# Side fetches from lists of byte offsets, read 32 at a time, in a graph network on one core

## The chip, the cores and the metric

The kernel runs on 1 core of one Trainium2 chip. The metric is the device time of one execution in microseconds (us); the kernel before takes 12477.9 us, the median of 3 runs (12459.53 to 12489.42).

## The reference

`h = relu(layernorm(x))` for 12500 nodes of 96 features. Then two mean aggregations over 200000 edges sorted by destination, two edge-conditioned maximum convolutions, and residual additions:

```python
def mean_agg(x):                       # twice; result 0.5*n1 + 0.5*n2, added to x
    return segment_sum(x[src], dst, N) * inv_deg
def _egnn_conv(x, src, dst, edge_attr, W_msg, W_edge, W_root, b):      # twice, with leaky_relu
    msg = x[src] @ W_msg + edge_attr @ W_edge
    agg = segment_max(msg, dst, N)     # 0 where a node has no edge
    return agg + x @ W_root + b
```

Each of the four aggregations needs `x[src]`: 200000 gathered rows of 384 bytes.

## The kernel before, in words

Four rounds follow each other: rounds 0 and 1 are sums, rounds 2 and 3 maxima. A round reads its node table from DRAM (`tables[r]`, 12544 rows of 96 float32), and ends with a stage over the nodes that writes the next table. Edges stand in 391 groups (`GROUPS`) of 512: 4 batches (`GRP`) of 128, one edge per partition.

**The main fetch.** GpSimd (POOL in the profile) issues one indirect DMA per batch (L449), 4 per group: 128 rows by 128 indices of `src_sb`, into a ring `rows` of 8 groups (`RING`). Group g waits until group g - 8 has been consumed (`used`, L441): in a sum when its windows are picked (`picked`), in a maximum when its rows are in PSUM (`rows_ps`). Group g of the ring stands on seat g % 8.

**The consumers.** TensorE takes the groups in order. In a sum it multiplies them with one-hot matrices (L681), and VectorE adds the results to `comp` (L927). In a maximum it multiplies with an identity (L702) on top of the edge features (L700), VectorE scans (L942), TensorE transposes and picks (L713, L724).

**The side fetch.** Some groups don't go through GpSimd: the table `ASIDE` names them. SyncE (SP, side buffer 0) and in the sums also ScalarE (ACT, side buffer 1) fetch each of a group's 512 rows by a DMA of its own (L296) from an address in a register. In `side_rows`, `numbers` (L319) loads 4 row numbers of one partition into registers, and each DMA's address is worked out from one of them. A side buffer holds one group, so the next side group of a queue is begun only when its last one is picked: `side_sums` waits for `picked` and then issues all 512. `PLAN` (9, seat) gives one side group per queue in 9 sweeps of 8 groups: groups 74, 146, 218, 290 and 362 for SP in a sum, 75, 147, ... for ACT, 72, 144, ... for SP in a maximum: 5 of each. TensorE waits for them in `gathered` (L665).

**The last rows.** The edges of the last, partial batch (`REST` = 64 rows) are fetched by SP in `tail_rows` (L302), one number and one DMA at a time, before its first side group of the round.

**SP's other work.** In a sum it stores the table (`store_table`), in a maximum it also loads flags and edge features by units of 4 groups into two buffers (`load_units`, L367 and L369), and side rows are issued between the units. Unit u waits for the scan that frees its buffer.

Of the kernel before, what the change touches and what calls it, by code (L numbers as in the profile page):

```python
# [10 lines left out]
U32 = mybir.dt.uint32  # L31
ALU = mybir.AluOpType
# [14 lines left out]
PLAN = {r: {0: (9, 2), 1: (9, 3)} for r in (0, 1)} | {r: {0: (9, 0)} for r in (2, 3)}  # L47
# [5 lines left out]
SIDES = {r: {e: (SWEEPS - 1) // span for e, (span, _) in PLAN[r].items()} for r in PLAN}  # L53
ASIDE = {r: {(b + 1) * PLAN[r][e][0] * RING + PLAN[r][e][1]: (e, b) for e in PLAN[r] for b in range(SIDES[r][e])} for r in PLAN}
# [14 lines left out]
PREP_ALL = 18  # L69
PREP_MAX = 22  # L70
assert CHUNK * CHUNKS == TILES and CHUNKS % 2 == 0 and RING == 2 * UNIT and UNIT < LAST < RING
assert GRP * (GROUPS - 1) < WHOLE and REST > 0
assert min(seat for _, seat in PLAN[0].values()) >= 2 and all(g < GROUPS - 1 for r in ASIDE for g in ASIDE[r])
# [33 lines left out]
def gnn(nc, x, srcs, cur, prev, nxt, cur_r, prev_r, eat, wm1, we1, wr1, b1, wm2, we2, wr2, b2, out):  # L107
    with ExitStack() as ctx:
# [13 lines left out]
        tables = [nc.dram_tensor(f"table{r}", (NPAD, D), F32).ap() for r in range(ROUNDS)]  # L122

# [14 lines left out]
        base = sb("base", [1, COLS], I32)  # L138
# [93 lines left out]
        side_in = {(r, e): [sem(f"side_rows_landed_{r}_{e}_half{k}") for k in range(2)] for r in rounds for e in PLAN[r]}  # L232
# [40 lines left out]
        def sweeps(engine, r, body):  # L273
# [3 lines left out]
            def passed(i):  # L277

                return {seat: sum(g // RING < i and g % RING == seat for g in ASIDE[r]) for _, seat in PLAN[r].values()}

# [10 lines left out]
        def side_rows(engine, r, e, b, p):  # L291

            span, seat = PLAN[r][e]
            at = bass.ds(b * (span * RING * GRP) + (span * RING + seat) * GRP, GRP)
            for k, row in enumerate(numbers(engine.engine, src_sb[p:p + 1, at], N - 1)):
                engine.dma_start(side[p:p + 1, e, k, 0:D], tables[r][bass.ds(row, 1), :]).then_inc(side_in[r, e][k % 2], 16)  # L296

        def tail_rows(engine, r):

            for p in range(REST):  # L300
                row, = numbers(engine.engine, src_sb[p:p + 1, WHOLE:WHOLE + 1], N - 1)
                engine.dma_start(tail[p:p + 1, 0, 0:D], tables[r][bass.ds(row, 1), :]).then_inc(tail_in, 16)  # L302

        def side_sums(engine, r, e):

            for s in range(2):
                engine.wait_ge(tstored[r][s], 16 * (CHUNKS // 2))
            if e == 0:
                engine.wait_ge(prep, PREP_ALL)
                tail_rows(engine, r)  # L310
            span, seat = PLAN[r][e]
# [15 lines left out]
        def _(sp):  # L327
# [21 lines left out]
            sp.dma_start(next_i, nxt).then_inc(s_next, 16)  # L349

# [10 lines left out]
            def load_units(r):  # L361
# [15 lines left out]
                span, seat = PLAN[r][0]  # L377
                units = 2 * span
                with sp.Fori(0, SIDES[r][0]) as b:
                    sp.wait_ge(rows_ps[r], b * (span * RING) + (seat + 1))  # L380
                    for t in range(units):
                        unit(b * span + (1 + t // 2), t % 2, UNIT)
                        for p in range(t * P // units, (t + 1) * P // units):
                            side_rows(sp, r, 0, b, p)
                with sp.Fori(SIDES[r][0] * span + 1, SWEEPS - 1) as i:
                    for u in range(2):
                        unit(i, u, UNIT)
# [743 lines left out]
```

## Time and profile before

| What | us |
|---|---|
| median of 3 runs | 12477.9 |
| span of the profiled execution, first to last instruction | 8075.9 |
| median less span | 4402.0 |
| GpSimd busy | 5983.3 |
| TensorE busy | 5063.4 |
| VectorE busy | 3315.1 |
| ScalarE busy | 1517.2 |

The page has no time for the profiled execution other than its span, so what lies around it is known only as the difference to the median. Busy times leave out the issue of DMAs by SP and ACT; those rows are marked SPq and ACTq and come from the queries by line. A round's start is seen in GpSimd's rows: the rounds begin at 57.8, 2035.9, 4047.2 and 6072.0 us.

### The profile page before, as it was taken

Reading aid. Unit: us, or ns where it says so; the run is one execution under the profiler, and the core shown is the slowest. Engines: PE = TensorE matmul, PEld = TensorE weight load, DVE = VectorE, ACT = ScalarE, POOL = GpSimd, SP = SyncE. Lnnn points to the kernel's source line nnn. Section 1 sums busy time; section 2 is a strip of 40 time slices with the busy share of each in tenths; the row PEclk is TensorE's granted clock in tenths of the full one; section 3 lists DMA queues with packets and bytes.
Section 4 is the critical chain, followed back from the end, with each engine's and each line's share of the span. In section 5 each row is a group of like instructions: output and inputs, shape, how many; then the busy total and the mean of one; then the engine's idle time right before and its main releaser. Section 6 shows DMA issues by size and latency. Waiting matters only on the chain.

```text
span 8075.9 us, 156597 instructions
## 1 busy us (share of the span) xinstructions
PE 5063.4 (63%) x26211; PEld 3792.9 (47%) x26211; DVE 3315.1 (41%) x7073; ACT 1517.2 (19%) x5246; POOL 5983.3 (74%) x6410
## 2 busy tenths in 40 slices
PE   3444444445444444444677888787787788878878
PEld 2333333334333333333555655565575565556556
DVE  5444444445433333333533433333343343333335
ACT  2000000001000000000322333333342333333334
POOL 6777777776777777777677777777767777777776
PEclk7555555556555555555677888888797787888888
DMA  3111111111211111111144434444433443444443
GB/s 92 42 42 41 42 41 42 41 41 46 57 42 42 41 42 41 41 41 41 41 94 93 98 89 96 93 98 93 92 72 92 97 98 87 97 93 97 93 92 79
DMA packets 337350, 553.38 MB, mean 69 GB/s; under 512 B 212648, under 2 KB 212648, under 8 KB 311848
## 3 DMA queue, kind: packets, MB, share of 16 engines
q0 software_dynamic: 196096, 301.60, 18.2%
q1 hardware_dynamic: 129796, 243.57, 11.9%
q14 instruction: 601, 4.92, 0.2%
q10 hardware_dynamic: 10788, 2.16, 0.2%
q8 instruction: 69, 1.13, 0.1%
HBM read 521.97 MB, written 24.87 MB: 68 GB/s over the span
## 4 chain that ended last, share of the span: by engine, by line
POOL 53%; issue 21%; PE 11%; SPq 9%; DMA 3%; DVE 2%; ACT 1%; DVEq 0%; ACTq 0%; POOLq 0%
POOL rows L449 53%; SPq L296 5%; SPq L319 3%; PE ps L702 3%; PE ps L700 3%; DMA rows<-table,src_sb 2%; PE ps L724 2%; PE ps L807 1%; SPq L302 1%; PE ps L713 1%; DMA arena<-in_eat 1%; PE ps L681 0%; PE ps L818 0%; ACT arena L493 0%; DMA table<-arena 0%
## 5 line engine op out<-in xcount | busy, mean ns | idle before, releaser
L449 POOL DMA_INDIRECT rows<-table,src_sb x6128 | 5790.9, 945 | 1958.6 <-issue 1849.1
L681 PE MATMUL ps<-arena,rows 128*98 128x128 f32 (+1 forms) x6088 | 1513.6, 429 | 2097.1 <-DMA rows<-table,src_sb 1446.2
L681 PEld LDWEIGHTS ps<-arena,rows 128*98 128x98 f32 (+1 forms) x6088 | 1259.8, 276 | 2373.4 <-DVE comp L927 1990.2
L942 DVE TENSOR_TENSOR_SCAN arena<-arena,ps 96x512 f32<-96x512 f32 x782 | 997.6, 1276 | 2433.9 <-PE ps L702 2409.3
L927 DVE TENSOR_TENSOR comp<-comp,ps 98x128 f32 (+1 forms) x3128 | 894.7, 286 | 2158.4 <-PE ps L681 1841.9
L700 PE MATMUL ps<-arena,we 32*96 32x512 f32 x1564 | 993.7, 719 | 765.1 <-DMA rows<-table,src_sb 415.9
L702 PEld LDWEIGHTS ps<-ident,rows 128*96 128x96 f32 x6168 | 823.5, 187 | 714.4 <-issue 714.4
L910 DVE TENSOR_TENSOR arena<-ps,meta 128x512 f32<-128x512 f32 x1564 | 1050.7, 672 | 29.2 <-issue 25.7
L518 ACT COPY comp<-ps 96x128 f32 x3128 | 818.8, 262 | 1057.6 <-PE ps L724 796.4
L702 PE MATMUL ps<-ident,rows 128*96 128x128 f32 x6168 | 1013.5, 316 | 0.0
L724 PE MATMUL ps<-arena 128*96 128x128 f32 x6256 | 932.8, 299 | 0.9 <-ACT arena L509 0.9
L724 PEld LDWEIGHTS ps<-arena 128*96 128x96 f32 x6256 | 829.0, 186 | 1.3 <-ACT arena L509 1.3
L509 ACT COPY arena<-ps 128x384 f32<-128x384 f32 x782 | 373.8, 478 | 1512.3 <-PE ps L713 1500.2
L700 PEld LDWEIGHTS ps<-arena,we 32*96 32x96 f32 x1564 | 210.2, 175 | 902.4 <-DMA rows<-table,src_sb 386.0
L590 ACT COPY arena<-comp 96x128 f32 (+1 forms) x392 | 83.6, 296 | 2064.3 <-issue 1896.1
L713 PE MATMUL ps<-ident,arena 96*128 96x96 f32 x3128 | 454.5, 275 | 0.2 <-DVE arena L942 0.2
L713 PEld LDWEIGHTS ps<-ident,arena 96*128 96x128 f32 x3128 | 392.0, 164 | 0.6 <-DVE arena L942 0.4
L598 ACT COPY rel_c<-node_rel 128x7 f32<-128x7 f32 (+1 forms) x42 | 8.3, 197 | 1742.6 <-issue 1741.4
L463 POOL TENSOR_SCALAR arena<-iota,rel_c 128x128 f32<-128x128 f32 x266 | 179.5, 690 | 123.6 <-ACT rel_c L598 77.8
L915 DVE TENSOR_TENSOR arena<-ps,meta 128x392 bf16<-128x392 f32 x391 | 216.9, 555 | 0.0
L687 PE MATMUL ps<-arena,ones_b 128*1 128x392 bf16 x391 | 185.9, 476 | 0.0
L807 PE MATMUL ps<-arena 128*128 128x96 f32 (+1 forms) x784 | 116.5, 309 | 29.2 <-POOL arena L463 9.3
(104 smaller groups left out, 1404.2 us busy)
## 6 DMA issues: line engine op xcount, KB each, us to landing
side<-table SPq DMA_DIRECT2D x10240, 0.4 KB
arena<-flags SPq DMA_DIRECT2D x194, 768.0 KB
rows<-table,src_sb POOLq DMA_INDIRECT x6128
side<-table ACTq DMA_DIRECT2D x5120, 0.4 KB
arena<-in_eat SPq DMA_DIRECT2D x194, 256.0 KB
table<-arena SPq DMA_DIRECT2D x56, 336.0 KB, 2.8
out<-xs SPq DMA_DIRECT2D x13, 336.0 KB
tail<-table SPq DMA_DIRECT2D x256, 0.4 KB
```

The costliest lines, as they stand in the source:

```text
L296: engine.dma_start(side[p:p + 1, e, k, 0:D], tables[r][bass.ds(row, 1), :]).then_inc(side_in[r, e][k % 2], 16)
L449: pool.indirect_dma_start(rows[:, g % RING, j, 0:D], None, tables[r][:, :], bass.IndirectOffsetOnAxis(src_sb[:, c:c + 1], 0)).then_inc(lan ...
L509: act.copy(runT[:, slot % SCANS].rearrange("p k d -> p (k d)"), ps[:, RUNT + slot % 2 * BANK:RUNT + slot % 2 * BANK + GRP * D]).then_inc(r ...
L518: act.copy(comp[0:D, bass.ds(at, P)], ps[0:D, WIN + slot % 2 * BANK + j * P:WIN + slot % 2 * BANK + (j + 1) * P]).then_inc(folded[r], 1)
L681: m = pe.matmul(ps[0:w, at + k * P:at + (k + 1) * P], got[k][:, 0:w], hot[:, j % HOTS, k, :], start=True, stop=True)
L700: pe.matmul(ps[0:D, at:at + W], we[D:P, r - 2, :], fe[D:P, u, q * W:(q + 1) * W], start=True, stop=False)
L702: m = pe.matmul(ps[0:D, at + k * P:at + (k + 1) * P], got[k][:, 0:D], ident[:, :], start=False, stop=(k == GRP - 1))
L713: m = pe.transpose(ps[:, at:at + D], run[:, slot % SCANS, k * P:(k + 1) * P], ident[0:D, 0:D])
L724: m = pe.matmul(ps[0:D, at:at + P], runT[:, slot % SCANS, k, :], hot[:, slot % HOTS, k, :], start=True, stop=True)
L910: dve.tensor_tensor(hot[:, slot % HOTS], ids.unsqueeze(1).to_broadcast([P, GRP, P]), rel, ALU.is_equal).then_inc(hot_ready[r], 1)
L927: dve.tensor_tensor(win, win, ps[0:w, of:of + P], ALU.add).then_inc(folded[r], 1)
L942: dve.tensor_tensor_scan(run[:, slot % SCANS], fe[0:D, slot // UNIT, q * W:(q + 1) * W], ps[0:D, ROWS + slot % 2 * BANK:ROWS + slot % 2 * ...
```

## The change

A new input `order` holds the same source numbers, one group of 512 per row. SP loads the rows of the side groups and of the last group into partitions 32 to 40, 64 to 71 and 96 to 101 of `low` (an SBUF tile; its partition 0 is the old `base`), and VectorE multiplies them by 384 in three instructions, so that they are byte offsets into the table. `side_rows` takes blocks of 32 offsets of one partition (consecutive edges, one batch of 128 at a time) in one load, and the DMA takes the register as it is, on a byte view of the table. `tail_rows` does the same with two blocks. The loops over the side groups are unrolled. The plan names more groups and closer together:

| | before | now |
|---|---|---|
| SP, each sum | 74, 146, ... 362 (5) | 50, 94, 140, 186, 234, 278, 324, 370 (8) |
| ACT, each sum | 75, 147, ... 363 (5) | 44, 90, 138, 182, 228, 274, 322, 366 (8) |
| SP, each maximum | 72, 144, ... 360 (5) | 60, 122, 186, 246, 308, 370 (6) |

The first side group of a round no longer waits for `picked`. In a maximum, the 16 blocks of a side group are spread over the units before it, and all stand ahead of the unit that holds the group.

```diff
-PLAN = {r: {0: (9, 2), 1: (9, 3)} for r in (0, 1)} | {r: {0: (9, 0)} for r in (2, 3)}
+BLOCK = 32
+PLAN = {r: {0: (48, 46, 8), 1: (44, 46, 8)} for r in (0, 1)} | {r: {0: (60, 62, 6)} for r in (2, 3)}
+SIDES = {r: {e: [g + max(0, 2 - g % RING) for g in range(first, first + step * n, step)] for e, (first, step, n) in PLAN[r].items()} for r in PLAN}
...
-        def side_rows(engine, r, e, b, p):
-            span, seat = PLAN[r][e]
-            at = bass.ds(b * (span * RING * GRP) + (span * RING + seat) * GRP, GRP)
-            for k, row in enumerate(numbers(engine.engine, src_sb[p:p + 1, at], N - 1)):
-                engine.dma_start(side[p:p + 1, e, k, 0:D], tables[r][bass.ds(row, 1), :]).then_inc(side_in[r, e][k % 2], 16)
+        def side_rows(engine, r, e, b, h):
+            k, p0 = h * BLOCK // P, h * BLOCK % P
+            at = LISTS[r, e] + b
+            for p, byte in enumerate(numbers(engine.engine, low[at:at + 1, h * BLOCK:(h + 1) * BLOCK], (N - 1) * (4 * D)), p0):
+                engine.dma_start(side[p:p + 1, e, k, 0:D].bitcast(U8), row_of(r, byte)).then_inc(side_in[r, e][k], 16)
...
+        def row_of(r, byte):
+            return table_bytes[r][bass.ds(byte, 4 * D)].rearrange("(a n) -> a n", a=1)
...
         def side_sums(engine, r, e):
             for s in range(2):
                 engine.wait_ge(tstored[r][s], 16 * (CHUNKS // 2))
+            engine.wait_ge(prep, PREP_ALL)
             if e == 0:
-                engine.wait_ge(prep, PREP_ALL)
                 tail_rows(engine, r)
-            with engine.Fori(0, SIDES[r][e]) as b:
-                engine.wait_ge(picked[r], b * (span * RING) + (seat + 1))
-                for p in range(P):
-                    side_rows(engine, r, e, b, p)
+            for b, g in enumerate(SIDES[r][e]):
+                if b:
+                    engine.wait_ge(picked[r], SIDES[r][e][b - 1] + 1)
+                for h in range(W // BLOCK):
+                    side_rows(engine, r, e, b, h)
...
+            for r, e in ((0, 0), (0, 1), (2, 0)):
+                for b, g in enumerate(SIDES[r][e]):
+                    at = LISTS[r, e] + b
+                    sp.dma_start(low[at:at + 1, 0:W], order[g:g + 1, :]).then_inc(s_lists, 16)
+            sp.dma_start(low[ENDING:ENDING + 1, 0:W], order[GROUPS - 1:GROUPS, :]).then_inc(s_lists, 16)
...
-                    if g >= RING:
-                        pool.wait_ge(used, (g - RING if g - RING not in ASIDE[r] else g - 2 * RING) + 1)
+                    before = g - RING
+                    while before in ASIDE[r]:
+                        before -= RING
+                    if before >= 0:
+                        pool.wait_ge(used, before + 1)
...
+            dve.wait_ge(s_lists, 16 * (len(ASIDE[0]) + len(ASIDE[2]) + 1))
+            for at, n in ((LISTS[0, 0], len(SIDES[0][0]) + 1), (LISTS[0, 1], len(SIDES[0][1])), (LISTS[2, 0], len(SIDES[2][0]))):
+                step(dve.tensor_scalar(low[at:at + n, 0:W], low[at:at + n, 0:W], float(4 * D), None, ALU.mult))
```

SP's program where it passes from the last rows to the first side group of round 0, before (`src_sb` holds row numbers, ISA is the arithmetic on registers):

```order
L319 TENSOR_LOAD src_sb
L302 ISA
L302 DMA tail<-table 1x96
L312 UNCONDITIONAL_BRANCH
L312 ISA
L319 ISA
L319 TENSOR_LOAD src_sb
L296 ISA
L296 DMA side<-table 1x96
L296 ISA
L296 DMA side<-table 1x96
```

The same place now (`low` holds byte offsets, sizes are in bytes):

```order
L312 TENSOR_LOAD low
L292 DMA tail<-table 1x384 x32
L312 TENSOR_LOAD low
L292 DMA tail<-table 1x384 x32
L312 TENSOR_LOAD low
L284 DMA side<-table 1x384 x32
L312 TENSOR_LOAD low
L284 DMA side<-table 1x384 x32
```

A load now stands ahead of 32 DMAs instead of 4, the register arithmetic between DMAs is gone, and so is the branch of the loop.

GpSimd's program through round 0 and into its node stage, before:

```order
L431 IOTA iota 128x128
L431 IOTA iota_b 128x128
L431 IOTA tile_at 128x98
L433 MEMSET comp 98x12672
L449 DMA rows<-table,src_sb 128x96 x1522
L463 TENSOR_SCALAR arena<-iota,rel_c 128x128 x6
```

And now (line numbers are those of the changed kernel):

```order
L439 IOTA iota 128x128
L439 IOTA iota_b 128x128
L439 IOTA tile_at 128x98
L441 MEMSET comp 98x12672
L460 DMA rows<-table,src_sb 128x96 x1498
L474 TENSOR_SCALAR arena<-iota,rel_c 128x128 x6
```

The count of its indirect DMAs falls by 24 in the round; in a maximum it falls from 1542 to 1538.

## Rows read from the trace of the kernel before
**Rows 1.** The page, busy time by engine: us (share of the span) xinstructions.

```profile
PE 5063.4 (63%) x26211; PEld 3792.9 (47%) x26211; DVE 3315.1 (41%) x7073; ACT 1517.2 (19%) x5246; POOL 5983.3 (74%) x6410
```

**Rows 2.** The page, the chain that ended last, by engine.

```profile
POOL 53%; issue 21%; PE 11%; SPq 9%; DMA 3%; DVE 2%; ACT 1%; DVEq 0%; ACTq 0%; POOLq 0%
```

**Rows 3.** Line L449, 100 to 1960 us: durations min/median/max, first and last start, idle time by releaser.

```profile
L449 POOL DMA_INDIRECT rows<-table,src_sb x1491: 940/944/961, 99.3 to 1959.5; - x187
...
  issue: 453.8, 1488
```

**Rows 4.** L449 by round, first and third: us, POOL busy (x), clock, DMA share, GB/s.

```profile
57.70:2035.80 1978.10, 1443.79 (x1522) 0.53 0.20 43
...
4047.20:6071.90 2024.70, 1454.94 (x1542) 0.83 0.40 92
```

**Rows 5.** Line L449, 57 to 100 us.

```profile
L449 POOL DMA_INDIRECT rows<-table,src_sb x28: 940/946/2500, 57.8 to 99.3; - x28
```

**Rows 6.** Line L296, 790 to 1088 us, SP's third side group of round 0.

```profile
L296 SPq FUSED_REGOPS  x512: 37/37/37, 791.4 to 1085.9; - x171
L296 SPq MOVE side<-table x512: 29/29/29, 791.4 to 1086.0; - x171
L296 SPq DMA_DIRECT2D side<-table x512: 224/225/364, 791.5 to 1086.0; - x171
```

**Rows 7.** Line L319, whole span, loads of registers.

```profile
L319 SPq TENSOR_LOAD <-src_sb x2816: 446/472/1070, 81.0 to 7877.4; - x188
L319 SPq FUSED_REGOPS  x2560: 51/51/72, 144.5 to 7877.3; - x197
...
L319 ACTq TENSOR_LOAD <-src_sb x1280: 312/516/751, 98.0 to 3772.2; - x183
...
L319 ACTq TENSOR_LOAD <-base x782: 304/309/327, 4073.7 to 8012.0; - x196
...
L319 ACTq TENSOR_LOAD <-node_base x56: 955/1548/2320, 1972.3 to 8054.2; - x56
```

**Rows 8.** Line L319, 2060.5 to 2061 us.

```profile
L319 ACTq TENSOR_LOAD <-src_sb x1: 312/312/312, 2060.7 to 2060.7; - x1
```

**Rows 9.** Timeline of ACT, 210.2 to 211.2 us: start, us, engine line op x.

```profile
210.23 1.01 ACTq L296 DMA_DIRECT2D side<-table  x3
```

**Rows 10.** Timeline of SP, 50 to 450 and 2025 to 2125 us.

```profile
55.40 0.45 SPq L349 DMA_DIRECT2D root<-in_nxt  x1
81.65 62.70 SPq L302 DMA_DIRECT2D tail<-table  x64
...
2054.88 63.62 SPq L302 DMA_DIRECT2D tail<-table  x64
```

**Rows 11.** Timeline of ACT, 2030 to 2062 us.

```profile
2032.98 0.27 ACT L562 CAST ps<-iota_b 128x128 f32<-128x128 bf16 x1 [9.57 <-DVE xs L1080]
```

**Rows 12.** Timeline of DVE, 96.8 to 102.1 us.

```profile
96.88 1.53 DVE L927 TENSOR_TENSOR comp<-comp,ps 98x128 f32 x4
98.32 0.68 DVE L910 TENSOR_TENSOR arena<-ps,meta 128x512 f32<-128x512 f32 x1
...
99.47 1.53 DVE L927 TENSOR_TENSOR comp<-comp,ps 98x128 f32 x4
```

**Rows 13.** The page, a matmul group, a DMA queue and a DMA issue.

```profile
q10 hardware_dynamic: 10788, 2.16, 0.2%
...
L681 PE MATMUL ps<-arena,rows 128*98 128x128 f32 (+1 forms) x6088 | 1513.6, 429 | 2097.1 <-DMA rows<-table,src_sb 1446.2
...
table<-arena SPq DMA_DIRECT2D x56, 336.0 KB, 2.8
```

**Rows 14.** Timeline of SP, 4090 to 4200 us, in a maximum.

```profile
4129.64 0.38 SPq L369 DMA_DIRECT2D arena<-in_eat  x1
4130.78 15.46 SPq L296 DMA_DIRECT2D side<-table  x28
```

**Rows 15.** Waits of PE: line, releaser, us in total, times, longest.

```profile
PE ps L700 <- DMA side<-table: 215.2, 10, 24.2
```

More of the change, by code:

```diff
@@ L68 @@
 PREP_START = 3
-PREP_ALL = 18
-PREP_MAX = 22
+PREP_ALL = 21
+PREP_MAX = 25
 assert CHUNK * CHUNKS == TILES and CHUNKS % 2 == 0 and RING == 2 * UNIT and UNIT < LAST < RING
 assert GRP * (GROUPS - 1) < WHOLE and REST > 0
-assert min(seat for _, seat in PLAN[0].values()) >= 2 and all(g < GROUPS - 1 for r in ASIDE for g in ASIDE[r])
+assert all(2 <= g % RING and RING <= g < GROUPS - 1 for r in ASIDE for g in ASIDE[r])
+assert all(len(ASIDE[r]) == sum(map(len, SIDES[r].values())) for r in ASIDE) and ENDING < 64
 assert 6 * COLS <= TILES * D and N < NPAD
@@ L231, in gnn @@
         tail_in = sem("tail_rows_landed")
-        side_in = {(r, e): [sem(f"side_rows_landed_{r}_{e}_half{k}") for k in range(2)] for r in rounds for e in PLAN[r]}
+        side_in = {(r, e): [sem(f"side_rows_landed_{r}_{e}_batch{k}") for k in range(GRP)] for r in rounds for e in PLAN[r]}
+        s_lists = sem("side_lists_in")
         landed = [sem(f"rows_landed_slot{k}") for k in range(RING)]
@@ L277, in passed @@
             def passed(i):
-                return {seat: sum(g // RING < i and g % RING == seat for g in ASIDE[r]) for _, seat in PLAN[r].values()}
+                return {seat: sum(g // RING < i and g % RING == seat for g in ASIDE[r]) for seat in range(RING)}
             body(0, RING, passed(0), {})
@@ L289, in sweeps @@
                 next_to = at + 1
-        def side_rows(engine, r, e, b, p):
-            span, seat = PLAN[r][e]
-            at = bass.ds(b * (span * RING * GRP) + (span * RING + seat) * GRP, GRP)
-            for k, row in enumerate(numbers(engine.engine, src_sb[p:p + 1, at], N - 1)):
-                engine.dma_start(side[p:p + 1, e, k, 0:D], tables[r][bass.ds(row, 1), :]).then_inc(side_in[r, e][k % 2], 16)
-        def tail_rows(engine, r):
-            for p in range(REST):
-                row, = numbers(engine.engine, src_sb[p:p + 1, WHOLE:WHOLE + 1], N - 1)
-                engine.dma_start(tail[p:p + 1, 0, 0:D], tables[r][bass.ds(row, 1), :]).then_inc(tail_in, 16)
+        def side_rows(engine, r, e, b, h):
[3 more added lines that the diff above has]
+                engine.dma_start(side[p:p + 1, e, k, 0:D].bitcast(U8), row_of(r, byte)).then_inc(side_in[r, e][k], 16)
+        def tail_rows(engine, r):
+            first = GRP * (GROUPS - 1)
+            for p0 in range(0, REST, BLOCK):
+                at = (WHOLE - first) * P + p0
+                for p, byte in enumerate(numbers(engine.engine, low[ENDING:ENDING + 1, at:at + BLOCK], (N - 1) * (4 * D)), p0):
+                    engine.dma_start(tail[p:p + 1, 0, 0:D].bitcast(U8), row_of(r, byte)).then_inc(tail_in, 16)
+        def row_of(r, byte):
+            return table_bytes[r][bass.ds(byte, 4 * D)].rearrange("(a n) -> a n", a=1)
         def side_sums(engine, r, e):
@@ L376, in load_units @@
                 tail_rows(sp, r)
[L377 to L385, printed above, removed]
+                t = 2
+                for b, g in enumerate(SIDES[r][0]):
+                    first = t
+                    if b:
+                        first = SIDES[r][0][b - 1] // UNIT + 1
+                        while t < first:
+                            unit(t // 2, t % 2, UNIT)
+                            t += 1
+                        sp.wait_ge(rows_ps[r], SIDES[r][0][b - 1] + 1)
+                    for t in range(first, g // UNIT):
+                        unit(t // 2, t % 2, UNIT)
+                        share = g // UNIT - first
+                        for h in range((t - first) * (W // BLOCK) // share, (t - first + 1) * (W // BLOCK) // share):
+                            side_rows(sp, r, 0, b, h)
+                    t = g // UNIT
+                if t % 2:
+                    unit(t // 2, 1, UNIT)
+                    t += 1
+                with sp.Fori(t // 2, SWEEPS - 1) as i:
                     for u in range(2):
@@ L655, in gathered @@
                         e, b = here[j]
[L656 to L657 removed]
+                        for k in range(GRP):
+                            pe.wait_ge(side_in[r, e][k], (b + 1) * (P * 16))
                         return [side[:, e, k] for k in range(GRP)]
```

23 lines of the change are left out of this document (12 added, 11 removed).

## The prediction

> **What bounds the kernel now.** I read the busy times first, then the chain, then the fetch line by itself. GpSimd is the busiest engine at 74% [rows 1] and holds 53% of the chain, with "issue" second [rows 2]. Its line tells why: between 99.3 and 1959.5 us it issues 1491 indirect DMAs, so one in 1860.2 / 1490 = 1.2484 us, of which 0.944 is the DMA and the rest idle time that nothing but its own issue ends (453.8 us over 1488) [rows 3]. A group of 4 takes 4.994 us. All four rounds have 1522 or 1542 such DMAs in about 2000 us [rows 4]: 6128 x 1.2484 = 7650 of the span's 8075.9 us are this metronome, the rest is the start and the node stages, which the change leaves alone. Consumers keep up: in the sums VectorE begins a group's additions at 96.88 and the next one's at 99.47, when rows are there, so 2.6 us per group [rows 12]. In the maxima TensorE waited 10 times for a side group, up to 24.2 us [rows 15], and GpSimd didn't notice, because it may run 8 groups ahead.
>
> So a DMA taken from GpSimd is worth 1.248 us, as long as the side group that replaces it comes no later than the ring covers. Those are the two terms.
>
> **What goes from GpSimd.** 24 DMAs in each sum, 4 in each maximum: 56 x 1.248 = 69.9 us off the span.
>
> **What a side group costs SP now.** Before, 512 rows were issued from 791.5 to 1086.0 us, 294.5 us, or 2.301 us per load of 4 numbers [rows 6]. In that are a load of 0.472 and its arithmetic of 0.051 [rows 7], and four times arithmetic 0.037, move 0.029 and DMA 0.225 [rows 6], together 1.687; the other 0.614 us lie between 14 instructions, 0.044 each. After, a row is move, DMA and two such gaps, 0.342 us, so 512 rows take 175.1 us, and to them come 16 loads of 32 numbers.
>
> That load stands nowhere in the trace. The bounds: a load of one number on SP costs no less than one of four (tail and side loads share the row, 446 at least, median 472), so 0.47 us is the lower end, if size costs nothing. At the upper end 7 numbers cost ACT 1.548 us, 0.221 each, or 7.1 us for 32. Between them: four numbers cost ACT 0.309 us from `base`, where no DMA stands ahead, and 0.516 behind DMAs [rows 7]; the one load of `src_sb` with none ahead took 0.312 [rows 8]. So some 0.2 us (0.16 on SP) is waiting behind a DMA, paid once per load, and four aligned numbers take 0.309. I take eight such pieces: 0.472 + 7 x 0.309 = 2.64 us, and with its gap 2.68. (Seven numbers at 0.955 at best are three such pieces, as an aligned 4 + 2 + 1 would be; the dearer ones of 1.548 start off a multiple of four, which lists of 32 never do.) Then 16 x 2.68 = 42.9, and the group takes 218.0 us to issue.
>
> The Trainium skill ("Runtime: NRT & Kernel Launch", Instruction fetch mechanics) puts a register load at about 200 ns per register even in bulk, which would be 6.4 us for 32. The row of seven numbers agrees with it (0.221 each), those of four do not (0.077 and 0.118), so I keep it as a rival.
>
> From the last issue to the pick come about 2 us of landing (an estimate below the 2.8 us of a table store) and four matmuls of 0.429 [rows 13], 3.8 us. The period of an SP side group is 221.8 us.
>
> **Against what it runs.** From group 50 to group 370 a sum has 320 groups, 14 of them aside, so GpSimd takes 306 x 4.994 = 1528 us for 7 periods, 218.3 each. SP falls behind by 3.5 us per period, 24.5 over seven.
>
> Where it starts: in round 1 SP begins the last rows at 2054.9 [rows 10]. They cost 63.6 us before and 2 x (32 x 0.342 + 2.68) = 27.2 now, so the first side group is picked at 2054.9 + 27.2 + 221.8 = 2303.9. GpSimd reaches its place at 2035.9 + 49 x 4.994 = 2280.6, and the pick would be due 6.1 us behind that (landing, two picks): 17 us late. The last is 41.7 late. The ring covers eight groups, 40.0 us, less those 6.1 and one pick at the consumers' pace of 2.6: 31.3 us. What is over, 10 us, is lost. In round 0 the first 28 DMAs took 41.5 instead of 33.7 us [rows 5], which shifts the due time to 316.4; SP starts at 81.65 + 2.1, its first is picked at 332.8, 16 late, and 9 us are lost. Together 19 us.
>
> ACT: three DMAs in 1.01 us give 0.390 per row [rows 9], less arithmetic and its gap 0.065 = 0.325. 512 of them are 166.4, sixteen dearer first ones about 4, sixteen loads of 0.516 + 7 x 0.309 + 0.03 = 43.3, and 3.8 at the end: 217.5, inside 218.3. It no longer waits for the first picks and starts right behind its copy at 2033 [rows 11]. It costs nothing; if its load is dearer, it falls behind as SP does, but has started 50 us earlier.
>
> **The rest.** Three VectorE instructions on 512 columns stand ahead of the first picks of round 0: at the 0.68 us of another one of 512 columns [rows 12] 2.1 us, of which I count all, though the ring may hide it. The 23 list loads cost SP 23 x 0.4 = 9 us [rows 14], from 55.9 us on; it was idle until 81.65 [rows 10], which hides them. In a maximum SP has 61 groups, 305 us, per side group: 218 us and 15 units whose two DMAs hold SP about 1.5 us (1.14 from the start of the second to the next side row, 0.4 for the first [rows 14]), 23 us. 64 us are spare, and the blocks now end about two groups before the due one; cost nothing. The DMA engines: ACT's queue held 0.2% of 16 engines' span for 5120 rows [rows 13], 8075.9 x 16 x 0.002 / 5120 = 0.05 us per row, while one comes every 0.17 us from both queues together; even on one engine that fits.
>
> Sum: 69.9 - 19 - 2 = 49 us. The profiled execution goes from 8075.9 to about 8027. The median of the runs is 4402 us above this span, and no row says what lies there. I take it as unchanged: 12477.9 - 49 = 12429, say 12430.
>
> **Rivals.**
> (a) Slower: the load is 3 to 3.8 us (0.118 each as SP's four cost, 3.76). Each 0.1 us adds 1.6 us to eight periods in two rounds, 25.6 us. From 2.83 us on the gain is gone; at 3.2 the kernel is 94 us slower, at 3.76 some 240: 12520 to 12720. For it: SP's own row has never shown 0.309. Against: the load with no DMA ahead [rows 8].
> (b) A load of 7.1 us: the period is 293, SP alone sets both sums: 4.46 x 256 = 1142 us of lateness, about 1090 us slower, 13570. By the figure of the Trainium skill's page named above it would be some 900 slower.
> (c) The load is between 2.73 and 2.93, and gain and lateness cancel within 0.2%.
> (d) What lies outside the span belongs to GpSimd's DMAs, slower when no profile is taken: 4402 / 6128 = 0.72 us more each. Then 56 x 1.97 = 110 us go and SP is never late: 12368. For it: nothing else is repeated 6128 times. Against: the profiled metronome is steady to 1%.
> (e) It belongs to the inputs. `order` adds 0.80 MB to about 35 MB of inputs and 5 of output, 2%, so 88 us more, against 49 gained: 12517.
> (f) The load costs hardly more than the four's. No lateness: 68 us gained, 12410; inside my forecast's own range.
>
> **Chances.** Forecast with (f) 0.48, own range 12405 to 12450; (d) 0.10; (c) 0.12; (a) 0.18; (e) 0.07; (b) 0.05. 0.2% is 25 us, about what a measurement of this kernel tells from no change. Faster 0.58, same 0.12, slower 0.30. The range goes from (d), 12365, to 12620, in the middle of (a); outside are (b) and the dearer half of (a), some 0.15, and little below.
>
> **What would show it.** GpSimd has 6072 indirect DMAs at 1.248 us. SP's load of 32 takes 2.6 us, ACT's 2.7, a row 0.34 and 0.33. Rows of GpSimd waiting for L681's successor would total about 20 us in the sums, late in each, and TensorE would wait for side groups 16 times a sum, up to 40 us. In the maxima its waits for side rows are gone. I am wrong if the load is above 2.8 us, if the move or the gaps grow, or if the difference between span and median moves.

## The result, and the profile after

The changed kernel takes 11748.9 us (median of 4 runs, 11742.27 to 11759.75), the kernel before 12471.4 us beside it (4 runs): the ratio is 0.9418 with a 95% interval of 0.9395 to 0.9441. The forecast was 12430, a gain of 48; the gain is 722.

The profiled execution of the changed kernel has a span of 11740.5 us and an own time of 11742.3, so 1.8 us lie around a span, not 4402. Busy time by engine (answers to [rows 1]):

```profile
PE 5690.6 (48%) x26211; PEld 4180.2 (36%) x26211; DVE 3307.3 (28%) x7076; ACT 1493.3 (13%) x5246; POOL 5935.1 (51%) x6354
```

GpSimd's work is what it was (5935 for 5983 us), its share fell from 74% to 51%, because the span is longer. The chain by engine and by line (answers to [rows 2]):

```profile
SPq 54%; issue 36%; PE 5%; another core or an unknown queue 2%; DVE 2%; DMA 1%; ACT 1%; DVEq 0%; ACTq 0%; POOL 0%; POOLq 0%
SPq L284 45%; SPq L312 7%; SPq L292 1%; PE ps L712 1%; PE ps L710 1%; PE ps L734 1%; DMA arena<-in_eat 1%; PE ps L817 1%; SPq L367 1%; PE ps L691 0%; SPq L365 0%; DVE comp L940 0%; PE ps L723 0%; PE ps L828 0%
```

Not GpSimd but SP's queue bounds this execution. GpSimd's fetch, 100 to 1960 us, with what ended its idle time (answers to [rows 3]):

```profile
L460 POOL DMA_INDIRECT rows<-table,src_sb x904: 938/945/961, 100.1 to 1904.9; - x181
...
  PE ps L691: 534.5, 18
  issue: 248.7, 815
  remote: 169.3, 71
```

904 DMAs where there were 1491: each takes what it took, but GpSimd stands idle behind TensorE ("remote" is an end of idle time that the profile can't name), and TensorE stands idle behind side rows (whole span: us in total, times, longest):

```profile
PE ps L691 <- DMA side<-table: 2376.2, 26, 150.3
```

The fetch of the first and of the third round (us, POOL busy (x), granted clock, DMA share, GB/s; answers to [rows 4]):

```profile
57.00:3183.00 3126.00, 1421.27 (x1498) 0.55 0.11 26
...
6564.00:9046.00 2482.00, 1452.10 (x1538) 0.70 0.30 72
```

The fetch of the first sum takes 3126 us and that of the first maximum 2482, for 1908 and 1927 in the profile before. SP's third side group, and GpSimd's DMAs in the same stretch (answers to [rows 6]):

```profile
L284 SPq MOVE side<-table x512: 3/29/1407, 884.7 to 1252.8; - x171
L284 SPq DMA_DIRECT2D side<-table x512: 2/228/765, 884.8 to 1252.8; - x171
```

```profile
884.00:1254.00 370.00, 166.20 (x176) 0.56 0.10 25
```

The medians are as in [rows 6], but a MOVE lasted up to 1.41 us instead of always 29 ns. Such long instructions, of about 0.70 us or twice that, are called halts here. The trace of the kernel before that the prediction was read from has none; another execution of the same kernel, run e5 below, has them.

### The profile page after: what moved, and what is told of

Its sections match the earlier page's. It is cut to its first block, busy times and chain, and to the rows that moved or that the text cites. A ratio compares the mean times of both kernels' runs of the same rounds, so it can differ in the third digit from the quotient of the medians.

```text
span 11740.5 us, 146003 instructions
## 1 busy us (share of the span) xinstructions
PE 5690.6 (48%) x26211; PEld 4180.2 (36%) x26211; DVE 3307.3 (28%) x7076; ACT 1493.3 (13%) x5246; POOL 5935.1 (51%) x6354
## 3 DMA queue, kind: packets, MB, share of 16 engines
q10 hardware_dynamic: 16932, 3.35, 0.2%
## 4 chain that ended last, share of the span: by engine, by line
SPq 54%; issue 36%; PE 5%; another core or an unknown queue 2%; DVE 2%; DMA 1%; ACT 1%; DVEq 0%; ACTq 0%; POOL 0%; POOLq 0%
SPq L284 45%; SPq L312 7%; SPq L292 1%; PE ps L712 1%; PE ps L710 1%; PE ps L734 1%; DMA arena<-in_eat 1%; PE ps L817 1%; SPq L367 1%; PE ps L691 0%; SPq L365 0%; DVE comp L940 0%; PE ps L723 0%; PE ps L828 0%
## 5 line engine op out<-in xcount | busy, mean ns | idle before, releaser
L691 PE MATMUL ps<-arena,rows 128*98 128x128 f32 (+1 forms) x5992 | 1380.4, 404 | 2351.5 <-DVE comp L940 1942.8
L691 PEld LDWEIGHTS ps<-arena,rows 128*98 128x98 f32 (+1 forms) x5992 | 1154.2, 259 | 2595.6 <-DVE comp L940 1760.6
L710 PE MATMUL ps<-arena,we 32*96 32x512 f32 x1564 | 1165.9, 833 | 478.6 <-DMA arena<-in_eat 423.1
L734 PE MATMUL ps<-arena 128*96 128x128 f32 x6256 | 1178.5, 350 | 443.6 <-issue 280.9
L712 PEld LDWEIGHTS ps<-ident,rows 128*96 128x96 f32 x6152 | 970.7, 215 | 918.4 <-issue 918.3
L712 PE MATMUL ps<-ident,rows 128*96 128x128 f32 x6152 | 1200.2, 353 | 45.8 <-issue 45.0
L691 PE MATMUL ps<-arena,side 128*98 128x128 f32 (+1 forms) x256 | 63.5, 429 | 2391.0 <-DMA side<-table 2376.2
L734 PEld LDWEIGHTS ps<-arena 128*96 128x96 f32 x6256 | 1032.5, 224 | 486.5 <-issue 479.1
L691 PEld LDWEIGHTS ps<-arena,side 128*98 128x98 f32 (+1 forms) x256 | 53.5, 278 | 2400.1 <-issue 2400.1
L723 PE MATMUL ps<-ident,arena 96*128 96x96 f32 x3128 | 535.2, 310 | 136.4 <-DVE arena L955 87.5
L723 PEld LDWEIGHTS ps<-ident,arena 96*128 96x128 f32 x3128 | 448.5, 186 | 171.3 <-DVE arena L955 96.9
```

The costliest lines, as they stand in the source:

```text
L691: m = pe.matmul(ps[0:w, at + k * P:at + (k + 1) * P], got[k][:, 0:w], hot[:, j % HOTS, k, :], start=True, stop=True)
L710: pe.matmul(ps[0:D, at:at + W], we[D:P, r - 2, :], fe[D:P, u, q * W:(q + 1) * W], start=True, stop=False)
L712: m = pe.matmul(ps[0:D, at + k * P:at + (k + 1) * P], got[k][:, 0:D], ident[:, :], start=False, stop=(k == GRP - 1))
L723: m = pe.transpose(ps[:, at:at + D], run[:, slot % SCANS, k * P:(k + 1) * P], ident[0:D, 0:D])
L734: m = pe.matmul(ps[0:D, at:at + P], runT[:, slot % SCANS, k, :], hot[:, slot % HOTS, k, :], start=True, stop=True)
```

## Experiments

Executions that were timed together have halts throughout or none at all, so each kernel is compared with the kernel before timed beside it: near 12590 us with halts (12471 in the first measurement), near 8076 without. Which kind comes can't be chosen, so the same kernel stands below more than once. It isn't the chip: one chip ran e13 and e14 with halts and e15 without.

**Without halts (e0, e1, e2, e9 to e12, e15)**

*e0: the kernel before, no edit.*

> The kernel before, unchanged, for a profile whose time is one of its timed runs. Theory R (the given profile is of an execution that had none of the 0.7 us halts seen in the changed kernel's trace, while the timed runs had them): the span is about 12460 us, and long MOVE and FUSED_REGOPS rows (0.7 us) stand in it. Theory S (the kernel before has a part of 4400 us outside its span, which the change removed): the span is about 8076 us beside a time of 12470.

Measured: 8074.1 us, span 8072.4. Neither theory's case came: the span is S's, but the time is the span's too. Nothing of 4402 us lies outside the span. The step "taken as unchanged" was wrong about what it is: the timed runs and the profiled one were not of one kind.

*e1: the changed kernel without side groups (with fewer preparation steps to count and no lists to multiply but the last rows').*

```diff
-PLAN = {r: {0: (48, 46, 8), 1: (44, 46, 8)} for r in (0, 1)} | {r: {0: (60, 62, 6)} for r in (2, 3)}
+PLAN = {r: {0: (48, 46, 0), 1: (44, 46, 0)} for r in (0, 1)} | {r: {0: (60, 62, 0)} for r in (2, 3)}
```

> The changed kernel without side groups: GpSimd fetches all 391 groups of every round (6248 indirect DMAs and 64 last rows per round by SyncE). Theory R1 (the halts come where SyncE's and ScalarE's single-row DMAs meet GpSimd's): almost no halts are left, 6248 x 1.249 + 430 = about 8230 us, far below both kernels. Theory R2 (halts come with GpSimd's indirect DMAs alone, or are a state of the chip): as many halts per us as before, 12000 us or more.

Measured: 8223.3 us, 6248 DMAs of GpSimd. Its line, 100 to 1960 us:

```profile
L460 POOL DMA_INDIRECT rows<-table,src_sb x1491: 940/944/957, 99.3 to 1959.2; - x187
...
  issue: 454.4, 1491
```

The same 1491 DMAs end at the same time as in [rows 3]: 1.248 us each, whatever SP does beside them. 120 DMAs more cost 149 us, 1.24 each. The first term of the forecast holds here. On halts the run says nothing, since the kernel before beside it (8076.9) had none either.

*e2: the new plan's code with the old number of groups (5, 5, 5).*

```diff
+PLAN = {r: {0: (74, 72, 5), 1: (75, 72, 5)} for r in (0, 1)} | {r: {0: (74, 72, 5)} for r in (2, 3)}
```

> The changed code (byte offsets, 32 per load, unrolled) with 5 side groups per queue and round, every 72 groups as before (from group 74 and 75). Theory R1: halts only while side rows are issued; SyncE needs some 365 us per side group against 355 to 360 us of GpSimd's time between them, so about 5 x 365 per sum and 9500 to 11500 us in all, below the changed kernel's 11745. Theory P (my prediction's: the count taken from GpSimd sets the gain): above the changed kernel by 56 x 1.25 = 70 us.

Measured: 8073.2 us, span 8071.5, 0.9 less than e0; both theories were about executions with halts, and this had none. SP's loads of 32 numbers (the line also has the tail's):

```profile
L312 SPq TENSOR_LOAD <-low x328: 2025/2062/3513, 82.3 to 7824.0; - x164
```

2.06 us, not 2.64; a side group is issued in 200.5 us, not 218.0 (294.5 before). The cheaper rows alone bring nothing: SP had slack. The Trainium skill ("Runtime: NRT & Kernel Launch", Instruction fetch mechanics) gives about 200 ns per register even in bulk, for loads that a table of the same page calls loads from HBM. These come from SBUF, and this trace shows 64 ns each.

*e9: the changed kernel, no edit.*

> The changed kernel, timed a third time, on whatever chip comes. Where the executions have no halts (the kernel before near 8075), the prediction's own working holds: 14 side groups fewer for GpSimd in the four rounds, near 8007 to 8040, ratio 0.992 to 0.996. Where they have halts (the kernel before near 12590), 11890 again, ratio 0.945, and the profile shows the rounds 3168, 3196, 2518 and 2528 us again. Rival: the chip is not what decides, and a chip that ran one kernel with halts runs another without.

Measured: 8050.1 us beside 8076.9, ratio 0.9967 (0.9955 to 0.998). 0.33%, a gain of 26.7 us, a little less than the 0.992 to 0.996 expected. Its span is 8045.1. Fetch line, 100 to 1960 us; then idle time of the whole line; then SP's third side group, ScalarE's first, and the tail in SP's timeline (start, us):

```profile
L460 POOL DMA_INDIRECT rows<-table,src_sb x1468: 938/944/961, 100.2 to 1959.8; - x184
...
  issue: 437.1, 1432
  PE ps L691: 38.6, 36
```

```profile
  issue: 1815.9, 5952
...
  PE ps L691: 66.5, 68
```

```profile
L284 SPq MOVE side<-table x512: 29/29/29, 545.5 to 747.3; - x171
L284 SPq DMA_DIRECT2D side<-table x512: 227/228/320, 545.5 to 747.4; - x171
```

```profile
L284 ACTq DMA_DIRECT2D side<-table x512: 234/235/479, 85.6 to 291.9; - x171
```

```profile
85.42 23.44 SPq L292 DMA_DIRECT2D tail<-table  x64
```

SP is not late (groups of 201.9 us; the 64 last rows with their two loads took 25.7 us, from 83.2 to 108.9, where 27.2 were forecast), but GpSimd did wait for TensorE: 66.5 us, 1.8 in the kernel before. The chain, 280 to 340 us (start, us, what), says for whom:

```profile
291.89 14.77 DMA side<-table
306.90 2.01 PE ps L691 x8
308.94 2.12 ACTq L312
```

ScalarE's last row is issued at 291.89 and lands 14.77 us later; the forecast allowed 2. The period of ScalarE's side groups is 225 us (they start at 85.6, 311.1, 537.1, ... 1661.9), against 44 groups of GpSimd in 219.7.

*e10: row numbers in the lists instead of byte offsets, so that each row has its address arithmetic again.*

```diff
-step(dve.tensor_scalar(low[at:at + n, 0:W], low[at:at + n, 0:W], float(4 * D), None, ALU.mult))
+step(dve.tensor_scalar(low[at:at + n, 0:W], low[at:at + n, 0:W], 1.0, None, ALU.mult))
-engine.dma_start(side[p:p + 1, e, k, 0:D].bitcast(U8), row_of(r, byte)).then_inc(side_in[r, e][k], 16)
+engine.dma_start(side[p:p + 1, e, k, 0:D], tables[r][bass.ds(byte, 1), :]).then_inc(side_in[r, e][k], 16)
... (tail_rows likewise)
```

> The changed kernel, but its lists hold row numbers instead of byte offsets, so that each row has the address arithmetic back (one FUSED_REGOPS more, three instructions a row instead of two); the loads of 32 and the plan stay. Theory, with halts: they are paid for each instruction of a sequencer while GpSimd issues. SP's side group is then 440 to 455 us in the sums instead of 371 (between the 371 of 2.03 instructions a row and the 468 of 3.25), and the time 13700 to 14000. Rival, it was the load of 4 numbers that cost: the group stays at 371 to 390 and the time at 11890 to 12100. Without halts both give 19 us more for a group that has slack: 8010 to 8060.

Measured: 8505.4 us, far outside. SP's third side group:

```profile
L284 SPq FUSED_REGOPS  x512: 37/37/37, 620.5 to 866.2; - x171
L284 SPq MOVE side<-table x512: 29/29/29, 620.6 to 866.2; - x171
L284 SPq DMA_DIRECT2D side<-table x512: 224/225/333, 620.6 to 866.3; - x171
```

A group is issued in 245.8 us, where e9 took 201.9: the arithmetic costs its 37 ns and more than that in gaps, 0.086 us a row. The expectation had counted 0.037. With the turn-round a period is 252 us against GpSimd's 219.7, SP bounds both sums, and these take 2126.8 and 2121.6. That is the slope that rival (a) described, reached from another side.

*e11: side groups in the maxima only.*

```diff
+PLAN = {r: {0: (48, 46, 0), 1: (44, 46, 0)} for r in (0, 1)} | {r: {0: (60, 62, 6)} for r in (2, 3)}
```

> The changed kernel without side groups in its two sums (GpSimd fetches them all), with its six for SyncE in each maximum. With halts: the sums take the 2240 us that they took without any side groups and the maxima stay at 2520, so 11888 - 1876 = about 10010. Rival: side groups in one round burden the others too (the queues, the memory), then over 10300. Without halts: 8223 - 2 x 30 = about 8163.

Measured: 8162.7 us, as expected.

*e12: in the sums only SP's eight.*

```diff
+PLAN = {r: {0: (48, 46, 8), 1: (44, 46, 0)} for r in (0, 1)} | {r: {0: (60, 62, 6)} for r in (2, 3)}
```

> The changed kernel without ScalarE's eight side groups in the sums; SyncE keeps its eight there and its six in the maxima. With halts: if SyncE's halts come from GpSimd alone, its group keeps 371 us and the sums stay near 3170 to 3200, the time near 11890. If ScalarE's queue brings some of SyncE's halts, the group goes towards the 340 of the maxima, the sums to 2750 to 2950, the time to 11100 to 11500. Without halts: 8 x 4 DMAs of GpSimd more in each sum, 8007 + 2 x 40 = about 8090.

Measured: 8086.0 us, as expected. GpSimd waited 1.5 us for L691 in all. So the 66.5 us of e9 come with ScalarE's groups beside SP's. The DMA queues between 150 and 250 us (packets, MB, share of 16 engines), of e9, of e10, of e12:

```profile
q1 hardware_dynamic: 471, 0.09, 3.2%
q10 hardware_dynamic: 463, 0.09, 3.1%
```

```profile
q10 hardware_dynamic: 428, 0.08, 0.5%
q1 hardware_dynamic: 418, 0.08, 0.5%
```

```profile
q1 hardware_dynamic: 509, 0.10, 0.6%
```

A row has two packets, its data (384 bytes) and its signal (4 bytes). In e9 both queues together moved 934 packets in 100 us, 4.67 rows in a microsecond; in e10 846 packets (4.23 rows), in e12 509. By their shares a packet took 0.11 us in e9 and 0.02 in the others, although the rows of e9 and e12 are the same.

SP and ScalarE issue 512 / 201.9 + 512 / 206.3 = 5.0 rows in a microsecond in e9: more than leaves, and the rest queues up. The packets' own times show the queue grow. From the issue of a row to the start of its data packet it takes 0.9 us for ScalarE's first row, 6.2 for its 300th and 11.9 for its last, and SP's rows beside them have up to 11.5; in e10 it stays between 0.8 and 1.2 us for the same places of both queues, in e12 between 0.8 and 1.0. So the two queues together have a limit between 4.2 and 5.0 rows in a microsecond, and ScalarE's rows reach it in the changed kernel.

What is full isn't shown. The Trainium skill ("DMA: Bandwidth & Descriptors", Why a DMA increments its semaphore by 16 and not by 1) says that a DMA from these queues uses the lowest-numbered of the 16 engines, and that each engine it uses posts one signal; with one signal per row, as this trace has it, all side rows would share one engine. In e9 the shares of both queues, 6.3% of 16 engines, add up to 1.01 of one. But packets overlap: laid over each other they cover only 0.60 of those 100 us, and an engine's number isn't in the trace.

*e15 (and e13): each row written as two halves, for two engines.*

```diff
-return table_bytes[r][bass.ds(byte, 4 * D)].rearrange("(a n) -> a n", a=1)
+return table_bytes[r][bass.ds(byte, 4 * D)].rearrange("(p a n) -> p a n", p=1, a=2)
-engine.dma_start(side[p:p + 1, e, k, 0:D].bitcast(U8), row_of(r, byte)).then_inc(side_in[r, e][k], 16)
+engine.dma_start(side[p:p + 1, e, k, 0:D].bitcast(U8).rearrange("p (a n) -> p a n", a=2), row_of(r, byte)).then_inc(side_in[r, e][k], 16)
... (tail_rows likewise)
```

> The changed kernel, each row of 384 bytes described as two runs of 192 on both sides, so that its DMA can be given to two DMA engines; instructions and plan as they are. Theory: all single rows of both queues go through one DMA engine, and that takes 4.7 of them in a microsecond (0.213 us each), while SyncE and ScalarE issue 5.0; the last rows of ScalarE's group land 19 us behind their issue, its period is 225.4 us instead of 212.6, and GpSimd waits 35 and 19 us in the sums. With two engines, without halts: the period 213, GpSimd's halts gone, 8045 - 50 = about 7995, ratio to before 0.990. Rival: the rows are not split, or an engine isn't what is full: 8045 again and the period 225; or two descriptors make each row's issue dearer, then the groups take over 220 us to issue and the time goes up to 8100 or more. With halts SyncE issues 1.4 rows in a microsecond and nothing is full: 11890 as before it.

> Rows in two halves once more, for a chip without halts: ScalarE's period 213 us instead of 225, GpSimd's 35 and 19 us of waiting in the sums gone, about 7995 beside 8050, ratio to before 0.990. Rival: the engine isn't what is full, or each row's issue gets dearer: 8045 or more. With halts 11890 again.

Measured: e13, with halts, 11895.1, ratio 0.9441 (0.9415 to 0.9466); e15, without, 8046.8, ratio 0.9964 (0.9952 to 0.9976), as e9. But ScalarE's queue has 16932 packets in e9, e13 and e15 alike: the rows weren't split. So neither shows anything of the limit, and whether a second engine would lift it was not tested.

**With halts (e3 to e8, e13, e14, e16, e17)**

*e3 and e8: the changed kernel, no edit.*

> The changed kernel again, timed beside the kernel before. Where the kernel before takes about 8077 us (no halts): SyncE's side group of 512 rows took 200 us to issue with the 5-group plan, under the 218 us that GpSimd leaves, so no lateness grows, GpSimd is the only bound, and 56 indirect DMAs go: 8077 - 70 = 8007 us, ratio 0.991. Where the kernel before takes about 12470 us (halts): ratio 0.942 as in the first comparison.

> The changed kernel on the same chip as the other three. Without halts 8077 - 70 = about 8007 us (its side group takes SyncE 200 us of 218). With halts about 11750 to 11900.

Measured: e3 11895.8 beside 12587.2, ratio 0.9454 (0.9438 to 0.947); e8 11888.0 beside 12587.6.

*e5: the kernel before, no edit.*

> The kernel before on the chip of this call. If the kernel before takes 12.5 ms here, theory H (on such a chip SyncE and ScalarE get through only some 1.8 and 2.2 instructions per us while GpSimd issues indirect DMAs, whatever the instruction is, and at full speed while it doesn't) expects: 0.7 us halts on MOVE and FUSED_REGOPS, SyncE's side group at about 0.57 rows per us beside GpSimd and 1.7 beside an idle GpSimd, both sums set by SyncE's queue. Theory G (every engine is slower there, whatever runs beside it) expects rates that don't depend on GpSimd. If it takes 8.08 ms, none of it.

Measured: 12594.7 us, span 12593.0. So the kernel before, traced with halts, fills the time of its timed runs. Wherever the span of a timed run is on record, from e0 to e17, it lies within 3 us of the run's time. The fetch line, 100 to 1960 us (to be laid beside [rows 3]), its rounds, and its sequencers at 1000 us:

```profile
L449 POOL DMA_INDIRECT rows<-table,src_sb x882: 942/947/967, 99.3 to 1959.5; - x177
...
  PE ps L681: 602.7, 14
  issue: 242.7, 795
```

```profile
57.00:3212.00 3155.00, 1447.51 (x1522) 0.56 0.12 26
6600.00:9500.00 2900.00, 1457.88 (x1542) 0.68 0.27 62
```

```profile
L296 ACTq DMA_DIRECT2D side<-table x1: 720/720/720, 999.3 to 999.3; - x1
L296 SPq FUSED_REGOPS  x1: 700/700/700, 1000.0 to 1000.0; - x1
L296 SPq MOVE side<-table x1: 702/702/702, 1001.4 to 1001.4; - x1
L296 SPq DMA_DIRECT2D side<-table x1: 700/700/700, 1002.8 to 1002.8; - x1
```

The last rows show the thing itself: instructions of 29, 37 and 225 ns take 0.70 us each. SP and the others stand still in pieces of 0.70 us, and nearly only while GpSimd issues indirect DMAs. Counted in steps of 5 us in the sums, SP issues 1.7 rows in a microsecond where GpSimd is idle and 0.44 to 0.49 where it issues (theory H: 1.7 and 0.57); in e8 2.4 and 0.8. That speaks for H's picture and against G. In e5 SP's side groups take 486 to 594 us in the sums. The waits in the maxima of e5, and below them those of e8 (us in total, times, longest):

```profile
POOL rows L449 <- PE ps L702: 1631.2, 293, 46.8
...
PE ps L700 <- DMA arena<-in_eat: 1015.7, 119, 34.6
```

```profile
POOL rows L460 <- PE ps L712: 743.2, 200, 23.7
...
PE ps L710 <- DMA arena<-in_eat: 504.4, 59, 26.1
```

*e6, e17: no side groups (the edit of e1).*

> The changed kernel with no side groups. On a chip where the kernel before takes 12.5 ms, theory H: SyncE and ScalarE are quiet in the sums, GpSimd keeps 1.25 us there, each sum about 2030 us; in the maxima the consumers decide; 8300 to 9500 us in all, far faster than both kernels. Theory G: slower than the changed kernel, since GpSimd at the changed kernel's pace of 1.6 us has more to issue: 12000 or more. Without halts 8223 as before.

> No side groups at all, timed: with halts 9583 beside 12590, ratio 0.76; without 8222 beside 8076, ratio 1.018. Rival: the one look at 9583 was an odd execution, and its median is nearer to the changed kernel's 11890.

Measured: e6 9583.0, just above the 8300 to 9500 of theory H and far from G's 12000 (a sum's fetch takes 2250 us, where H had 2030); e17 9583.5 beside 12593.1, ratio 0.7613 (0.76 to 0.7626). GpSimd's line in e17:

```profile
L460 POOL DMA_INDIRECT rows<-table,src_sb x6248: 938/944/2747, 58.8 to 9486.2; - x196
...
  issue: 1716.2, 5625
...
  PE ps L691: 4.1, 12
```

With halts the version without side groups is by far the fastest of all, and GpSimd's wait for TensorE's picks in the sums is gone (4.1 us); without halts it is the slowest but e10 (8223). GpSimd's own extra time comes in single pauses: between 100 and 2200 us its DMAs start 1.25 us apart as ever, except that one in sixteen starts some 4.3 us after the one before it, behind idle time that ends in "remote". What ends it isn't known.

*e7: the edit of e2.*

> The changed code with 5 side groups per queue and round. On a chip with 12.5 ms for the kernel before, theory H: a side group costs SyncE some 370 us and there are 5 instead of 8, so a sum takes about 5 x 370 plus what GpSimd needs behind it, 2200 to 2500 instead of 3130 us: 10000 to 10700 in all, under the changed kernel. Theory P (more taken from GpSimd is the gain): above the changed kernel. Without halts 8073.

Measured: 10468.3 us, inside theory H's 10000 to 10700, but by luck: a side group took 478 us where 370 were expected, and the sums 2609 and 2656 where 2200 to 2500 were. The new rows with the old number of groups are 2126 us faster than e5, and the changed kernel, with its groups added, is 1420 slower than this.

The fetch of the four rounds takes 2608, 2656, 2372 and 2358 us; in e8 3168, 3196, 2518 and 2528; in e5 3153, 3194, 2891 and 2879. Against e5, e8 gains 723 us in the maxima and loses 17 in the sums. Against e7, its three more groups per engine in a sum cost 560 and 540 us, and its sixth group in a maximum 146 and 170. Here e7's third group of SP, and GpSimd's DMAs beside it:

```profile
L284 SPq DMA_DIRECT2D side<-table x512: 2/225/1393, 1107.5 to 1584.8; - x171
```

```profile
1106.00:1586.00 480.00, 264.83 (x280) 0.56 0.14 30
```

*e4: the new plan with the old side rows (loads of 4, arithmetic); the last rows stay new.*

```diff
-for p, byte in enumerate(numbers(engine.engine, low[at:at + 1, h * BLOCK:(h + 1) * BLOCK], (N - 1) * (4 * D)), p0):
-    engine.dma_start(side[p:p + 1, e, k, 0:D].bitcast(U8), row_of(r, byte)).then_inc(side_in[r, e][k], 16)
+g = SIDES[r][e][b]
+for p in range(h * P // (W // BLOCK), (h + 1) * P // (W // BLOCK)):
+    for k, row in enumerate(numbers(engine.engine, src_sb[p:p + 1, g * GRP:(g + 1) * GRP], N - 1)):
+        engine.dma_start(side[p:p + 1, e, k, 0:D], tables[r][bass.ds(row, 1), :]).then_inc(side_in[r, e][k], 16)
```

> The changed plan (8, 8 and 6 side groups) with the old way of a side row: 4 row numbers per load, arithmetic on registers per DMA, unrolled. Without halts SyncE needs 295 us per side group against 218 of GpSimd's: (295 + 4 - 218) x 7 less what the ring covers, about 530 us lost per sum, so 8077 + 1060 - 70 = 9070 us. Rival: the plan alone gives the gain and the way of a row is worth nothing: 8007. With halts, SyncE's time per row decides: slower than the kernel before.

Measured: 14310.0 us, slower than the kernel before, as expected with halts. The new plan alone, with halts, would have cost 1720 us; the cheap rows give it back and 700 more. The fetch of a maximum takes 3012 and 2960 us here, 494 and 432 more than with the new rows in e8, and more than in e5: so it is the rows that made the maxima faster, not the plan.

*e14: the edit of e10.*

> The kernel with the address arithmetic back in each row, once more, for a chip with halts. With them: SyncE's side groups take 440 to 455 us in the sums and the time is 13700 to 14000 if halts are paid per instruction, 371 to 390 and 11890 to 12100 if the load of 4 numbers was what cost. Without them 8505 again.

Measured: 13513.1 us, the groups in the sums 423 us on average. SP's third:

```profile
L284 SPq FUSED_REGOPS  x512: 3/37/797, 1011.6 to 1442.6; - x171
...
L284 SPq DMA_DIRECT2D side<-table x512: 3/225/729, 1011.7 to 1442.7; - x171
```

Both expectations missed (440 to 455 and 371 to 390 us). That only the load of 4 was dear falls clearly. But the arithmetic costs 53 us a group with halts and 44 without: SP doesn't pay by the instruction either.

*e16: seven of ScalarE's groups in the sums.*

```diff
+PLAN = {r: {0: (48, 46, 8), 1: (52, 51, 7)} for r in (0, 1)} | {r: {0: (60, 62, 6)} for r in (2, 3)}
```

> The changed kernel with 7 side groups for ScalarE in the sums, every 51 groups, instead of 8 every 46. Theory: the two queues together land 4.7 single rows in a microsecond, so 8 + 8 groups of 512 rows need 218 us of each 220, and ScalarE's come late; with 244 us for a period of ScalarE nobody is late. Without halts the fetch of a sum is then 1501 DMAs x 1.249 = 1875 us instead of 1905 and 1889, and the time 8045 - 44 = about 8000, ratio to before 0.990 to 0.992. Rival: what GpSimd waited for was not the rate but single late groups anyway, then the 4 DMAs more per sum cost 5 us each and the time is 8055. With halts SyncE's 8 groups set the sums: 3170 us and 11890 as before.

Measured, with halts: 11880.5 beside 12593.1, ratio 0.9426 (0.9404 to 0.9448), the sums 3169 and 3189. As expected: with one group of ScalarE less nothing changes, so ScalarE doesn't set the sums. The run was made for the case without halts, where it would test whether the limit of the two queues is what costs e9 its waits. That wasn't seen, and stays open.

**What the halts cost.** Mean of SP's side groups in the sums, their issue without halts, and GpSimd's DMAs that fall beside one:

| | with | without | DMAs beside | us more per DMA |
|---|---|---|---|---|
| e8, e16 (new rows, 8) | 370 | 201 | 171 | 0.98 |
| e7 (new rows, 5) | 478 | 201 | 274 | 1.01 |
| e14 (arithmetic, 8) | 423 | 246 | 168 | 1.05 |
| e4 (old rows, 8) | 465 | 294 | 172 | 0.99 |
| e5 (old rows, 5) | 571 | 294 | 263 | 1.05 |

In the sums each indirect DMA of GpSimd stops SP for about 1.0 us, whichever of these rows SP issues. In the maxima it is less: from row to row SP takes 0.66 us in e8 and 0.33 in e9, which makes 0.81 us for each of GpSimd's DMAs beside these rows (0.81 to 0.84 in e4, e5, e7 and e8; counted the same way 1.04 to 1.12 in their sums). Why, no run shows.

From the 1.0 us the sums come out: SP's own work (tail and groups with their turn-round), and 1 us for each of GpSimd's DMAs. After: 27 + 8 x 207 + 1498 x 0.98 = 3151, measured 3168; before: 64 + 5 x 298 + 1522 x 1.05 = 3152, measured 3153; e7: 27 + 5 x 207 + 1522 x 1.01 = 2599, measured 2609. The 1.0 was read from the same runs, so this describes them; no run was forecast with it. It also counts the DMAs before SP's first group and after its last as if they stopped SP.

## Why the prediction was wrong

- **The step that failed** is "The median of the runs is 4402 us above this span, and no row says what lies there. I take it as unchanged". It lies inside the span of the executions that were timed, as halts; the profiled one had none. Everything worked out from it was a sum for another kind of execution. The timed runs of the kernel before in the first measurement have no trace, so this is inferred: e5 fills that time, e0 doesn't, and 1.7 us lie outside either. The prediction had named the sign, "if the difference between span and median moves": it is 1.8 us in the trace after.
- That the kernel got faster, as forecast, is luck as far as the sum goes: it had 10 of its 69.9 us in the maxima, where all of the gain came from, and the rest in the sums, where none came.
- Rival (d), "What lies outside the span belongs to GpSimd's DMAs", had the place nearly right (a cost per DMA of GpSimd) and the payer wrong: halts add 1360 us where SP has no side rows (e17 against e1) and 4520 to the kernel before (e5 against e0). It forecast 110 us where 722 went.
- Where the 722 come from: the maxima (e8 against e5: 373 and 350 us), by the cheaper rows (e4). There, before, SP's loads of edge features stood behind side rows: TensorE waited 1015.7 us for them at L700 and GpSimd 1631.2 for L702. After, these waits are 504.4 and 743.2. For the maxima "64 us are spare" and "cost nothing" were right without halts and far off with them.
- The sums gained nothing: "24 DMAs in each sum" went, but SP bounds them, its own work grew from 1554 to 1683 us, and 24 DMAs less stop SP for only 24 us less. That would make each sum 105 us longer; 15 and 2 were measured, and the difference is that a DMA stops SP for 0.98 us and not 1.05, which nothing here explains.
- **By its own terms, without halts** (e9 against e0): "56 x 1.248 = 69.9 us" is right (e1, e11, e12). The four fetches fell from 7657.7 to 7632.3 us, by 25.4, so 44 went into waits where the sum had 19 + 2.
- "a side group costs SP ... 218.0 us" was mis-sized, it is 201.9: the load takes 2.06 to 2.12 us (medians of e2 and e9) and not 2.64, so SP is never late, and the lateness forecast for it doesn't exist.
- ScalarE "costs nothing" was wrong, by the term "about 2 us of landing": 14.8. Behind it stands "even on one engine that fits", with 0.05 us per row from a trace in which 3.3 rows left in a microsecond and none queued. At 5.0 issued, one leaves every 1 / 4.67 = 0.214 us and they queue. The 19 us of SP's lateness didn't come and 44 of waits with ScalarE's groups did (e12 has none of them), which left 27 us of the 49.
- Rivals (a), (b) and (c) about a dearer load fell with e2; (e), the inputs, fell with e0.

## What to carry to other kernels

A difference of thousands of microseconds between a profile and the runs is the first thing to explain: the profile may show another kind of execution than the one that is timed, and then a gain worked out from it is for that kind only. When a second engine takes over small work from the one that paces, ask what it pays for that engine's activity (here SP lost 1 us per DMA of GpSimd, with halts), and whether all its small DMAs can leave: here two queues of single rows had one common limit. And a plan that is best in one kind of execution can be the worst in the other (no side groups: 9583 and 8223 us; this change: 11890 and 8050).

## What was not expected of the hardware

- Halts of 0.70 us on SP, ACT and DVE (its register arithmetic took up to 723 ns after, 71 in e9) beside GpSimd's indirect DMAs, about 1.0 us of SP's time per DMA in the sums and 0.8 in the maxima; GpSimd without side groups goes from 1.25 to 1.44 us per DMA in the sums on average (e1, e17). What makes them, and why the same chip shows them at one time and not five minutes later (e13, e15), is open: in every execution with a trace the time was the span and some 2 us, so the cost of recording can't be told from the chip's own.
- Single-row DMAs of two queues together leave at 4.67 in a microsecond when 5.0 are issued, and the last lands 14.8 us after its issue (e9); at 4.23 none is late (e10).
- A load of 32 registers from SBUF takes 2.06 to 2.12 us on SP and 2.24 on ScalarE, where 4 take 0.47 and 0.52 [rows 7].
